# A chunked recurrence with its round loop written out on every engine, constant wait values, and no helper increments on TensorE

## The reference

```
def step(S, inp):
    rt, wt, kt, vt, at, bt = inp
    sa = jnp.einsum('bhij,bhj->bhi', S, at)
    S = S * wt[:, :, None, :] + sa[:, :, :, None] * bt[:, :, None, :] + vt[:, :, :, None] * kt[:, :, None, :]
    yt = jnp.einsum('bhij,bhj->bhi', S, rt)
    return (S, yt)
```

## Time and profile before

| | us |
|---|---|
| median of three runs | 1676.69 |
| the three runs | 1676.69, 1677.48, 1669.33 |
| profiled execution, its own time | 1668.34 |
| its span | 1666.6 |
| TensorE busy in the span | 1424.1 (85%) |
| VectorE busy | 893.4 (54%) |
| ScalarE, GpSimd busy | 562.9, 170.8 |

### The profile page before, as it was taken

One profiled execution on the slowest core, in us unless ns is written; L12 is line 12 of the kernel. 1 busy time (PEld: TensorE's weight loads), 2 busy tenths in 40 slices (PEclk: granted clock), 3 DMA queues, 4 the chain that ended last, 5 costly groups with the idle time before them and its releaser, 6 DMA issues. The chain is left out here.

```text
span 1666.6 us, 34768 instructions
## 1 busy us (share of the span) xinstructions
PE 1424.1 (85%) x13272; PEld 788.3 (47%) x13272; DVE 893.4 (54%) x1708; ACT 562.9 (34%) x777; POOL 170.8 (10%) x366
## 2 busy tenths in 40 slices
PE   3879999999999964999999968875887877776998
PEld 2523333333333332555555533332776777665565
DVE  5377888888888424222222236876454554465221
ACT  2316777767777723111111105431111111101221
POOL 3220000000000030000000000222211221100000
PEclk9959999999999977999999989997889898887999
DMA  3301121121211030000000010000000000010000
GB/s 96 56 8 24 24 40 26 27 39 23 42 24 24 3 135 1 0 1 0 0 0 0 0 51 1 0 0 8 3 4 4 4 4 3 4 51 9 13 13 25
DMA packets 28819, 32.82 MB, mean 20 GB/s; under 512 B 11113, under 2 KB 20809, under 8 KB 28708
## 3 DMA queue, kind: packets, MB, share of 16 engines
q1 hardware_dynamic: 27940, 30.12, 8.4%
q10 hardware_dynamic: 768, 1.05, 0.2%
HBM read 14.18 MB, written 2.10 MB: 10 GB/s over the span
## 5 line engine op out<-in xcount | busy, mean ns | idle before, releaser
L655 DVE TENSOR_REDUCE at_block_max<-at_p_ring 128x4 f32<-128x512 f32 x576 | 367.7, 686 | 75.9 <-PE at_p_ring L561 41.7
L632 ACT ACTIVATE at_probs<-at_p_score,abias 128x1024 f32<-128x1024 f32 (+2 forms) x320 | 318.6, 1028 | 122.9 <-PE at_p_score L591 68.6
L561 PE MATMUL at_p_ring<-kt,qt 64*128 64x128 bf16 (+3 forms) x1152 | 187.0, 284 | 10.0 <-PEq L718 7.4
L606 PE MATMUL at_p_out<-at_probs,at_vs 128*32 128x512 f32 (+3 forms) x1536 | 164.3, 500 | 0.4 <-ACT at_probs L632 0.4
L1031 DVE TENSOR_TENSOR moe_prod<-moe_p_up,moe_act 128x512 f32<-128x512 f32 (+1 forms) x56 | 38.7, 691 | 222.0 <-PE moe_p_up L1003 222.0
L585 PE MATMUL at_p_score<-qt,kt 64*128 64x512 bf16 (+3 forms) x768 | 145.9, 331 | 5.7 <-ACT at_probs L632 4.8
L561 PEld LDWEIGHTS at_p_ring<-kt,qt 64*128 64x128 bf16 x1152 | 69.9, 96 | 130.3 <-DVE at_block_max L655 86.4
L1021 ACT ACTIVATE moe_act<-moe_p_gate 128x512 f32<-128x512 f32 (+1 forms) x56 | 33.4, 597 | 276.2 <-PE moe_p_gate L1003 276.2
L1003 PE MATMUL moe_p_gate<-xt_moe,w_gate 128*128 (+1 forms) x224 | 107.4, 602 | 3.8 <-PEq L2065 3.8
L990 PE MATMUL moe_p_down<-w_down,moe_hidden 128*128 128x256 f32 (+1 forms) x448 | 110.6, 391 | 0.0
L1003 PE MATMUL moe_p_up<-xt_moe,w_up 128*128 (+1 forms) x224 | 105.3, 592 | 0.0
(11 more groups left out here) (276 smaller groups left out, 2074.9 us busy)
## 6 DMA issues: line engine op xcount, KB each, us to landing
qt<-qparts SPq DMA_DIRECT2D x96, 64.0 KB, 2.4
kt<-kparts SPq DMA_DIRECT2D x96, 64.0 KB, 2.4
x<-in_x_dram SPq DMA_DIRECT2D x4, 512.0 KB, 8.7
out_dram<-x SPq DMA_DIRECT2D x4, 512.0 KB, 2.9
w_gate<-in_w_gate_dram SPq DMA_DIRECT2D x1, 1760.0 KB
w_up<-in_w_up_dram SPq DMA_DIRECT2D x1, 1760.0 KB
w_down<-in_w_down_dram SPq DMA_DIRECT2D x1, 1664.0 KB
qt<-qrows SPq DMA_DIRECT2D x16, 64.0 KB, 2.4
```

The lines of the kernel that those rows point to most:

```text
L561: mm = pe.matmul(bank[:, col:col + nb * P], qt[nxt][h * ROWS:(h + 1) * ROWS, pair, t * P:(t + 1) * P], kt[nxt][h * ROWS:(h + 1) * ROWS, pa ...
L606: mm = pe.matmul(p_out[32 * h:32 * h + 32, left(k):QC], vs[(now - e[2]) % BUFS][:, key, h, :], probs[g % PROBS][:, h % 2, at:at + w], star ...
L632: act.activation(probs[g % PROBS][:, :, 0:len(pairs) * w], p_score[g % 2][:, :, 0:len(pairs) * w], ACT.Exp, bias=abias[:, c * TPB + key:c ...
L655: dve.tensor_reduce(dst, src, AX.X, ALU.max).then_inc(s["fill_used"], 1)
```

## The change

The `Fori` loops of the recurrence become Python loops, so that every engine's list holds all eight rounds one behind the other. t is then always a plain number: each wait compares with a constant, addresses are constants, and the register instructions and branches are gone. The conditions that told round 0 by its type now tell it by its value. The semaphore `seen` and its increments on TensorE go, in `pe_wait` and in `ys`. The order of the stages and their operations stay as they are.

```diff
--- before.py
+++ after.py
@@ -1377,7 +1377,7 @@
         gh = [sb(f"gh{c}_", [P, EH, 2, RN]) for c in range(2)]
         state = [sb(f"state{c}_", [P, EH, RN]) for c in range(2)]
         made, dve_did, act_did, staged = sem("made"), sem("dve_did"), sem("act_did"), sem("staged")
-        y1_made, seen = sem("y1_made"), sem("seen")
+        y1_made = sem("y1_made")
         hop_made, hop_done, y_out = sem("hop_made"), sem("hop_done"), sem("y_out")
 
         def flat(t):
@@ -1392,14 +1392,12 @@
             if act:
                 pe.wait_ge(act_did[b], t * ACT_MARKS["each"] + ACT_MARKS[act])
 
-            pe.sem_inc(seen[b], 1)
-
         def hop_wait(eng, sem_, marks, t, b, name):
 
             eng.wait_ge(sem_[b], (t - 1) * marks["each"] + marks[name] + (sem_ is hop_done))
 
         def last(t):
-            return isinstance(t, int) and t == TPB
+            return t == TPB
 
         def decay_at(t, b, c):
             return ds(t * HALF_CHUNKS + (b * S // L + c), 1)
@@ -1413,8 +1411,8 @@
                             for b in range(B):
                                 stage(t, b)
                 run(0, True, False)
-                with eng.Fori(0, TPB - 1) as r:
-                    run(r + 1, False, False)
+                for t in range(1, TPB):
+                    run(t, False, False)
                 run(TPB, False, True)
             return program
 
@@ -1435,7 +1433,7 @@
             def _(pe):
                 def turn(t, b):
                     pe.wait_ge(staged[b], t + 1)
-                    if not isinstance(t, int):
+                    if t:
                         pe.wait_ge(dve_did[b], t * DVE_MARKS["each"])
                         pe.wait_ge(act_did[b], t * ACT_MARKS["each"])
                     for n, (a, c) in enumerate(((bt, kt), (ar, vt))):
@@ -1717,7 +1714,7 @@
                              bank[b][:, 2:4, 0:EH * L].rearrange("p c (h l) -> p h c l", h=EH)
                              ).then_inc(act_did[b], 1)
 
-                with act.Fori(0, TPB) as t:
+                for t in range(TPB):
                     for stage in (tok, w0, ta_, y_):
                         for b in range(B):
                             stage(t, b)
@@ -1752,7 +1749,7 @@
 
                 for b in range(B):
                     y1(0, b)
-                with pool.Fori(0, TPB - 1) as t:
+                for t in range(TPB - 1):
                     for b in range(B):
 
                         pool.wait_ge(made[b], t * PE_MARKS["each"] + PE_MARKS["a3"])
```

## The result

The changed kernel takes 1596.2 us (median of four, 1594.45 to 1596.86) against 1673.45 us for the kernel before (1669.33 to 1677.48): ratio 0.954, 95% interval 0.951 to 0.957. The profiled executions are 1668.34 and 1596.86 us, 71.5 apart.

What follows compares the result with a forecast made beforehand. TensorE sets the pace of the recurrence's rounds, with idle holes at the seams. Terms 24.1 + 10.5 + 0 + 4 + 1 + 0 = 39.6 us off 1668.3 give 1628.7, plus 4 for timed runs: 1633 us, range 1613 to 1656.

Steps and rivals of the forecast that it cites:

- (a): At the seams between rounds, six back-edges of TensorE's loop go, with their idle holes: 24.1 us gained.
- (b): After the seams, TensorE no longer starts rounds at the lower clock: 10.5 us gained, bounds 5 and 13.
- (c): TensorE's "issue" holes inside the rounds, 19.1 us, come from code streaming and stay: 0 us gained.
- (d): At TensorE's waits, without helper increments each real wait shortens by 0.06 to 0.08 us: 4 us gained.
- (e): Constant wait values instead of register arithmetic help only VectorE's state step: 1 us gained, bounds 0 and 2.
- (f): More code on VectorE, ScalarE, GpSimd costs 0; shifted code behind the recurrence 0, plus or minus 4 us.
- Rival 1: At the seams another wait takes the hole's place, or the hole isn't the jump's: 1667 us, chance 0.04.
- rival 3: In the written-out rounds straight code becomes bound by fetching, every block late: slower, 1750 us, chance 0.04.
- Rival 2: In the rounds straight code streams without holes, so inner holes go too: 61 us gained, 1611 us, chance 0.12.

Runs made afterwards that it cites:

- E1: Changed kernel with all 46 increments a round put back behind TensorE's waits, rounds still written out; 1644.2 us, ratio 0.981 to the kernel before.
- E5: Changed kernel with six artificial idle holes of TensorE at the start of rounds 2 to 7, without jumps or increments; 1642.6 us, ratio 0.984.
- E10: Changed kernel with 28 increments a round behind the waits of z, xz and zy, plus an increment in front of every wait; 1634.4 us.
- E9: Changed kernel with increments put back behind all waits but those of z, 36 of 46 a round; 1615.2 us, ratio 0.969.
- E6: Changed kernel with increments put back behind the waits of z, xz and zy alone, 28 a round; 1609.3 us, ratio 0.962.
- E7: Changed kernel with increments put back behind all waits except those of z, xz and zy, 18 a round; 1596.9 us, ratio 0.956.
- E4: Changed kernel with loops and registers put back on VectorE, ScalarE and GpSimd, only TensorE written out; 1598.2 us, ratio 0.957.
- E2: Changed kernel with all increments put back, but in front of TensorE's waits instead of behind them; 1599.4 us, ratio 0.958.

## Why the prediction was wrong

The mechanisms were named, but one was put at zero, another was credited to the seams alone, and the odds between forecast and second rival were wrong.

(a) *Back-edges*, 24.1 us: right. All seven seams run through, and E1, which is written out with everything else kept, gains 24.5 us.

(b) *The clock*, 10.5 us: right for six holes standing alone, 13.4 us by E5, but wrong in this sum, which takes the seams away and leaves the inner holes. That is what E1 does, and it gained 24.5 us, little more than the length of the seams' holes; its inner holes are 4.1 us longer, so at most some 4 us of clock can hide there, not 10.5. TensorE's busy time in the rounds (PE in these lines) shows why. In order: before, E1, E5, E10, changed:

```profile
sum 318.16, PE 253.37 PEld 236.20 DVE 165.35 ACT 41.37 POOL 50.76; mean PE 31.67 PEld 29.52 DVE 20.67 ACT 5.17 POOL 6.34
sum 293.73, PE 252.23 PEld 234.75 DVE 164.47 ACT 41.09 POOL 50.67; mean PE 31.53 PEld 29.34 DVE 20.56 ACT 5.14 POOL 6.33
sum 285.65, PE 242.27 PEld 226.43 DVE 164.30 ACT 67.65 POOL 50.99; mean PE 30.28 PEld 28.30 DVE 20.54 ACT 8.46 POOL 6.37
sum 285.11, PE 239.13 PEld 220.33 DVE 164.53 ACT 40.80 POOL 50.59; mean PE 29.89 PEld 27.54 DVE 20.57 ACT 5.10 POOL 6.32
sum 245.36, PE 229.31 PEld 213.35 DVE 163.54 ACT 40.80 POOL 50.63; mean PE 28.66 PEld 26.67 DVE 20.44 ACT 5.10 POOL 6.33
```

The same matmuls take 24.1 us longer before than after, and in E1, which has no seam hole, still 22.9. By the trace's clock records TensorE works for 40.3 us at the lower level before, 40.6 in E1, 34.9 in E5 and 4.9 in the changed kernel. At half the clock that is an estimated 18 us lost to it before, and as much in E1. In E1 the clock falls in or up to 1.2 us behind inner holes of 1.3 to 3.0 us. It is back where the inner holes shrink too: E9, with 9.0 us of them, is at 1.00 from round 1 on. Holes alone don't decide it: E10 has 29.5 us of them, none over 1.9, and a clock of 1.00 in six of eight rounds.

(c) *Holes inside the rounds*, "they come from code streaming, not from the loop. ... I leave this mix as it is: 0 us": **this is the step that failed.** The observation was right, since they aren't the loop's (E1), but the conclusion wasn't. Round 0 had the increments too, so it couldn't stand for the changed kernel: I had taken "written out" for "already changed". Measured: 19.2 us of holes gone, and with them nearly the whole price of the clock.

(d) *Increments*, 4 us: the direct price was about right, the whole price twelve times too small. The direct one is seen in the same place as in the earlier trace rows, Z on VectorE and then the weight load that waits for it, now after the change:

```profile
1219.55 0.41 DVE L1631 TENSOR_TENSOR rc_Z<-rc_bank,level_masks 128x256 f32<-128x256 f32 x1
```
```profile
1220.02 0.20 PEld L1477 LDWEIGHTS rc_bank<-rc_Z,rc_Y 64*64 64x64 f32 x4 [0.93 <-DVE rc_Z L1631]
```

Z ends at 1219.96 and the load starts at 1220.02: 0.06 us instead of 0.12. Over the rounds the waits themselves cost about 5 us: E6 and E7 added are 8.2, of which 3.3 are holes beyond those of the changed kernel. The other 40 us come only when all 46 stand together: the same instructions delay the fetch.

(e) *Constant values*, 1 us: within its bounds (E4, 1.6 us together with the loops of three engines); for TensorE alone no run shows them. (f) *More code*: right; outside the rounds 1348.4 and 1349.7 us.

Rival 1 (another wait takes the place) and rival 3 (straight code bound by fetching) fell: no new wait at the seams, and no holes at full speed. E1 and E10 show that rival 3's mechanism exists; it needs fetches that start late. Rival 2 was the one that came, by the reason given for it, that the sequencer gets further ahead once waits sit on the weight loads; its condition, that the jumps had thrown the fetched blocks away, fell with E1. It had 0.12, and its 61 us still missed 12 us of the 73 in the rounds, since it priced the clock for the seams alone and the waits at 4. The rest of the 77 us is in the timed runs of before, whose median lay 5 us above its profiled execution, while that of the changed kernel doesn't.

The account of the rounds: seams 24.1, inner holes 19.2, clock about 18 (the estimate in (b)), waits about 5 (E6 and E7 without their holes), together 66 of 72.8 us. No run isolates the remaining 6 to 7 us; TensorE's busy time is 9.8 us longer in E10 too, where the clock is up nearly throughout, so something beside the clock stretches it. A kernel with TensorE's loop kept and its waits directly on the small matmuls, which would be the fourth corner beside before, E1 and the changed kernel, wasn't tried.

## What to carry to other kernels

On an engine with short instructions, TensorE with 64 x 64 matmuls above all, look at where a wait sits. On the weight load itself it cost 0.06 us from the end of the awaited work to the load, on an instruction of its own in front 0.12 us (one pair of rows each), and enough of the latter went with late blocks of code. "Issue" holes of up to 3 us whose places lie multiples of 256 instructions apart, each ended 2 to 3 us after a packet of the instruction queue started, were late code here, and the cure was far from where they stood. Before a stretch of the old kernel is taken as a sample of the new one, check that it lacks every part that the change removes: here round 0 lacked TensorE's loop but still had the increments, and its holes went with them (E1 against the changed kernel).

## What was not expected of the hardware

Two delays that cost 7.1 and 1.1 us alone cost 39.7 us together (E6, E2, E10), and 18 and 28 blocking waits a round that cost 1.1 and 7.1 us cost 48.3 us together (E7, E6, E1): with 4.4 us from block to block and about 2.6 us from a packet's start to its use, the fetch has an estimated slack of under 2 us, and hardly a hole opens until it is used up.

The clock's price wasn't the sum of its causes either: six holes of 4.5 us alone cost 13.4 us on top (E5), but taking six of 3.7 to 4.3 us away and leaving the inner ones gave back only their length (before against E1). And 28 holes of up to 1.9 us, 29.5 us in all, lowered the clock hardly at all (E10), where 21 of up to 3.0 us, 23.5 in all, held it at 0.85 to 0.95 in six of eight rounds (E1).
